# Head of a graph-attention kernel: weight, adjacency and x transfers put in another order

## What is computed

```python
def _L0_gnn_ref(h, adj, W, a):            # h = layernorm(x), W 128x128, a 1x256
    Wh = jnp.einsum('bni,oi->bno', h, W)
    a1 = a[0, :OUT_F]
    a2 = a[0, OUT_F:]
    si = Wh @ a1
    sj = Wh @ a2
    e = jax.nn.leaky_relu(si[:, :, None] + sj[:, None, :], negative_slope=ALPHA)
    attention = jnp.where(adj > 0, e, NEG_INF)
    attention = jax.nn.softmax(attention, axis=-1)
    h_prime = jnp.einsum('bij,bjo->bio', attention, Wh)
    return jax.nn.elu(h_prime)
...
x = x + _L0_gnn_ref(_layernorm(x, axis=-1), adj, L0_gnn_W, L0_gnn_a)
x = x + _L0_ffn_ref(_layernorm(x, axis=-1), ...)   # router per batch, top 2 of 8 experts, gelu, W1, W2
```

## Time and profile before

| | us |
|---|---|
| median of 3 runs | 276.9 |
| lowest and highest run | 275.93, 277.78 |
| the profiled execution's own time | 276.77 |
| its span, first to last instruction | 275.0 |

### The profile page before, as it was taken

How to read it: one execution, slowest core, us unless ns; L and a number is a source line. 1 busy time by engine, 2 the same in 40 slices (tenths; PEclk the granted TensorE clock), 3 DMA queues, 4 the chain that set the end, 5 groups by cost and what they waited for, 6 DMA issues and landing times. The chain is left out here.

```text
span 275.0 us, 6287 instructions
## 1 busy us (share of the span) xinstructions
PE 250.4 (91%) x1872; PEld 222.7 (81%) x1874; DVE 231.0 (84%) x647; ACT 223.4 (81%) x511; POOL 153.6 (56%) x228
## 2 busy tenths in 40 slices
PE   6878988998899899999989789999999999999980
PEld 3557977898889888899979457999999999999980
DVE  5589999999999999999999774587777777777774
ACT  2467898999999999999999659669888888888731
POOL 3435197778876697787468711164433333344544
PEclk9999999999999999999999999999999999999996
DMA  6999566643565346541000014678555545453122
GB/s 99 195 237 215 109 99 114 109 77 76 88 114 97 66 76 112 76 60 19 4 0 4 0 49 163 191 180 282 193 175 166 179 158 182 163 169 99 42 76 78
DMA packets 40706, 31.57 MB, mean 115 GB/s; under 512 B 2416, under 2 KB 36624, under 8 KB 40672
## 3 DMA queue, kind: packets, MB, share of 16 engines
q1 hardware_dynamic: 31936, 21.72, 24.7%
q0 software_dynamic: 8736, 9.45, 23.3%
HBM read 27.48 MB, written 4.20 MB: 115 GB/s over the span
## 5 line engine op out<-in xcount | busy, mean ns | idle before, releaser
L1253 PE MATMUL banks<-whx,prob_t 128*128 128x129 f32 x512 | 67.7, 277 | 2.7 <-ACT h_att L977 2.5
L1253 PEld LDWEIGHTS banks<-whx,prob_t 128*128 128x128 f32 x512 | 61.7, 192 | 5.5 <-issue 5.4
L383 POOL TENSOR_SCALAR x_all<-x_all,rstd,nb 128x128 f32<-128x128 f32 x56 | 41.0, 743 | 2.9 <-POOL nb L372 2.7
L1131 ACT ACTIVATE logit<-logit,nb,rstd 128x128 f32<-128x128 f32 x60 | 24.8, 484 | 19.3 <-POOL nb L448 19.3
L1005 ACT ACTIVATE prob_t<-banks 128x512 f32<-128x512 f32 x64 | 38.0, 637 | 2.7 <-PE banks L1238 2.7
L1238 PE MATMUL banks<-ident,logit 128*128 128x128 f32 x256 | 36.9, 275 | 3.5 <-DVE logit L533 3.3
L443 POOL TENSOR_SCALAR veps<-mv 128x4 f32<-128x4 f32 x15 | 6.7, 448 | 51.6 <-DVE mv L837 51.6
L366 POOL TENSOR_TENSOR rstd<-var,minus_half 128x8 f32<-128x8 f32 (+1 forms) x20 | 34.8, 1738 | 0.4
L1238 PEld LDWEIGHTS banks<-ident,logit 128*128 128x128 f32 x256 | 29.0, 141 | 5.9 <-DVE logit L533 5.6
L1415 PEld LDWEIGHTS banks<-w2s,masked_even 128*128 128x128 f32 x256 | 29.8, 192 | 0.7
L1415 PE MATMUL banks<-w2s,masked_even 128*128 128x128 f32 x256 | 29.9, 275 | 0.0
(11 more groups left out here) (149 smaller groups left out, 569.6 us busy)
## 6 DMA issues: line engine op xcount, KB each, us to landing
adj_sb<-in_adj_dram POOLq DMA_DIRECT2D x16, 512.0 KB, 7.0
w_pair<-w_parts SPq DMA_DIRECT2D x30, 256.0 KB, 2.4
x_all<-in_x_dram SPq DMA_DIRECT2D x16, 256.0 KB, 3.1
w2r<-in_L_ffn_W_dram SPq DMA_DIRECT2D x32, 128.0 KB, 2.1
out_dram<-prob_t SPq DMA_DIRECT2D x15, 256.0 KB, 2.3
w_parts<-in_L_ffn_W_dram SPq DMA_DIRECT2D x1, 1024.0 KB, 7.3
b_mix<-b_spread POOLq DMA_DIRECT2D x1, 704.0 KB, 5.8
out_dram<-prob_t SPq DMA_DIRECT2D x4, 64.0 KB, 1.7
```

Source lines behind the costliest of these rows:

```text
L383: nc.gpsimd.tensor_scalar(x_all[:, b, tile], x1_all[:, b, tile], rstd12[c % 4][:, 1, t:t + 1], nb2[c % 2][:, t:t + 1], ALU.mult, ALU.add). ...
L1131: nc.scalar.activation(zn[par][:, tile], zs[par][:, tile], ACT.Identity, bias=nb3[par][:, t:t + 1], scale=rstd3[par][:, t:t + 1]).then_inc ...
L1253: last = nc.tensor.matmul(into[:, 0:D + 1], prob_t[:, t, c * P:(c + 1) * P], whx[b % 3][:, c, 2:WHX], start=(c == 0), stop=(c == T - 1))
```

## The change

1. `a_src` and `a_dst` become two columns of one tile `a_both`, loaded by one transfer of 128x2 single elements, and that transfer is SP's first, ahead of W.
2. POOL issues adj0 as its first instruction, ahead of the constants; `load_adj(0)` ahead of `norms(0)` goes.
3. SP issues x2 when the prepared weights are ready (`s_prep`) and no longer behind adj0's landing; x3 still waits for that.
4. W1's load moves from behind x5 to behind x7, the small loads from behind x7 to behind x9, and the four `split_w1_hi` on ACT from steps 4 to 7 to steps 6 to 9.
5. In DVE's hand-written start, logits(0, 0) comes ahead of mask(1), and logits(0, 1) ahead of the first maximum of batch 1.
6. PE: for batch 0 `spread_dst` waits for each tile of `whx` by itself and not for all four; the fillers go from 8 to 6 at the start and from 5 to 3 behind `project(0)`.

```diff
--- before.py
+++ after.py
@@ -57,8 +57,8 @@
         idle_in = sb("idle_in", [P, N], BF16)
         minus_half = sb("minus_half", [P, T])
         gnn_w_sb = sb("gnn_w_sb", [P, D])
-        a_src = sb("a_src", [P, 1])
-        a_dst = sb("a_dst", [P, 1])
+        a_both = sb("a_both", [P, 2])
+        a_src, a_dst = a_both[:, 0:1], a_both[:, 1:2]
         w_stats = sb("w_stats", [P, 6])
         w_mean = sb("w_mean", [P, 2])
         gnn_w_centred = sb("gnn_w_centred", [P, D])
@@ -266,20 +266,21 @@
                 sp.dma_start(b1_sb[:], b1).then_inc(s_rw, 16)
                 sp.dma_start(b2_sb[:], b2).then_inc(s_rw, 16)
 
+            sp.dma_start(a_both[:], gnn_a.rearrange("a (k d) -> d (a k)", k=2),
+                         allow_slow_non_contiguous=True).then_inc(s_gw, 16)
             sp.dma_start(gnn_w_sb[:], gnn_w).then_inc(s_gw, 16)
-            sp.dma_start(a_src[:], gnn_a[0:1, 0:D].rearrange("a d -> d a")).then_inc(s_gw, 16)
-            sp.dma_start(a_dst[:], gnn_a[0:1, D:2 * D].rearrange("a d -> d a")).then_inc(s_gw, 16)
             load_x(0)
             load_x(1)
+            sp.wait_ge(s_prep, 1)
+            load_x(2)
             sp.wait_ge(s_adj[0], 16)
-            load_x(2)
             load_x(3)
             for b in range(4, B):
                 sp.wait_ge(s_mask, b - 3)
                 load_x(b)
-                if b == 5:
+                if b == 7:
                     sp.dma_start(w1_parts[:, :, 1, :].bitcast(F32), w1.rearrange("e p f -> p e f")).then_inc(s_w1raw, 16)
-                if b == 7:
+                if b == 9:
                     load_small()
 
             def load_w1(b):
@@ -325,6 +326,7 @@
 
         @block.gpsimd
         def _(pool):
+            nc.gpsimd.dma_start(adj_sb[0][:], adj_dram[0]).then_inc(s_adj[0], 16)
             nc.gpsimd.memset(ident[:], 0.0).then_inc(s_ident, 1)
             pool.wait_ge(s_ident, 1)
             nc.gpsimd.affine_select(out=ident[:], in_=ident[:], compare_op=ALU.not_equal, fill=1.0, base=0,
@@ -398,7 +400,6 @@
                 if 0 <= n + 4 <= B - 1:
                     load_adj(n + 4)
 
-            load_adj(0)
             norms(0)
             load_adj(1)
             norms(1)
@@ -475,9 +476,9 @@
             for i in range(3):
                 nc.vector.memset(whx[i][:], 1.0).then_inc(s_dconst, 1)
 
-            dve.wait_ge(s_gw, 48)
+            dve.wait_ge(s_gw, 32)
             nc.vector.bn_stats(w_stats[:], gnn_w_sb[:]).then_inc(s_centre, 1)
-            nc.vector.tensor_scalar(a_src_scaled[:], a_src[:], 1.0 - ALPHA, None, ALU.mult).then_inc(s_centre, 1)
+            nc.vector.tensor_scalar(a_src_scaled[:], a_src, 1.0 - ALPHA, None, ALU.mult).then_inc(s_centre, 1)
             dve.wait_ge(s_centre, 1)
             nc.vector.bn_aggr(w_mean[:], w_stats[:]).then_inc(s_centre, 1)
             dve.wait_ge(s_centre, 3)
@@ -617,10 +618,10 @@
             shift_high(0)
             shift_low(0)
             stats1(2)
+            logits(0, 0)
             make_mask(1)
-            logits(0, 0)
+            logits(0, 1)
             masked_max(1, 0)
-            logits(0, 1)
             masked_max(1, 1)
             logits(0, 2)
             masked_max(1, 2)
@@ -1079,8 +1080,8 @@
             probs(1, 0)
             for n in range(1, B - 1):
                 step(n)
-                if 4 <= n < 8:
-                    split_w1_hi(n - 4)
+                if 6 <= n < 10:
+                    split_w1_hi(n - 6)
             probs(B - 1, 1)
             normalize(B - 2)
             exp_h(B - 2)
@@ -1207,10 +1208,12 @@
             def spread_dst(b):
 
 
-                pe.wait_ge(s_wh, T * b + T)
-                if b >= 1:
+                if b >= 1:
+                    pe.wait_ge(s_wh, T * b + T)
                     pe.wait_ge(s_md, T * b)
                 for t in range(T):
+                    if b == 0:
+                        pe.wait_ge(s_wh, t + 1)
                     last = nc.tensor.transpose(dst_ps[:, t * P:(t + 1) * P], whx[b % 3][:, t, 0:1].to_broadcast([P, P]),
                                                ident[:])
                 last.then_inc(s_dst, 1)
@@ -1281,18 +1284,18 @@
                     attend(n, 2)
 
             pe.wait_ge(s_dconst, 1)
-            keep_busy(8)
+            keep_busy(6)
             pe.wait_ge(s_dconst, 2)
             pe.wait_ge(s_const, 1)
             transpose_x(0)
-            pe.wait_ge(s_gw, 48)
+            pe.wait_ge(s_gw, 32)
             pe.wait_ge(s_centre, 4)
             nc.tensor.transpose(dst_ps[:, 2:D + 2], gnn_w_centred[:], ident[:])
-            nc.tensor.matmul(dst_ps[:, 0:1], gnn_w_centred[:], a_dst[:], start=True, stop=True)
+            nc.tensor.matmul(dst_ps[:, 0:1], gnn_w_centred[:], a_dst, start=True, stop=True)
             nc.tensor.matmul(dst_ps[:, 1:2], gnn_w_centred[:], a_src_scaled[:], start=True, stop=True).then_inc(s_prep_ps, 1)
             pe.wait_ge(s_prep, 1)
             project(0)
-            keep_busy(5)
+            keep_busy(3)
             spread_dst(0)
             transpose_x(1)
             keep_busy(2)
```

## The result

| | before | after |
|---|---|---|
| median of the runs, us | 276.75 (4 runs, 275.93 to 277.78) | 281.47 (4 runs, 280.45 to 284.46) |
| after / before | | 1.0175, 95% interval 1.0136 to 1.0214 |
| profiled execution, us | 276.8 | 281.57 |
| its span, us | 275.0 | 279.8 |
| mean granted TensorE clock | 0.992 | 0.986 |

The forecast was 275.2 us in a range of 273.9 to 277.6: wrong in size and in sign. Of the 4.8 us by which the profiled span is longer, 3.7 stand in the first 22 us.

The account below looks back on a forecast made before the run. VectorE was taken to bound the kernel, full from about 26 us, so only its start could gain. maximum(1,1) moving from 18.60 to 17.0 gave 1.6 us, other terms 0: 276.8 - 1.6 = 275.2 us, range 273.9 to 277.6.

Parts of the forecast that it names:

- The price: x0: First x load, now issued 0.92 us behind adj0: takes 3.9 us, landing at 5.6, 0.6 us later; ends 4.6 to 7.4.
- by turns: Queues alternating packet by packet on the DMA engines: x0 lands at 7.4 us, total 277.0 us instead of 275.2.
- the fillers, costed at nothing: TensorE's start: six fillers for eight end near 4.0 us, then idle until x0; cost put at nothing.
- (b): Rival at the first load: x0 starves behind adj0; 277.0 us for landing at 7.4, 278.4 for 8.8; chance 0.17.
- (c): Rival in batch 0: TensorE stays at its lower clock, 3.1 us more on the chain, 277.4 us total; chance 0.07.
- ScalarE does not bind: First batches: x1's leaky row comes at about 13.6 us, ahead of logits(0,0) at 14.2, so no wait.
- x0 + 11.4: Start of maximum(1,1): x0's landing plus 2.2, 7.3 (adj1's transfer) and 1.9 us, for x0 above about 5.2.
- adj0's issue: GpSimd's start: adj0 issued at 0.74 us in place of the identity's memset, 1.20 us sooner.
- x2's stall: VectorE's 1.11 us wait before x2's statistics: goes, as x2 lands near 10 to 12 us, needed at 13.4.
- adj1 as the next one late: At mask(1): adj1, issued at 7.8 us, lands at 15.1, and VectorE waits about 0.3 us.
- the merged weights: Sync's start: one transfer for two score columns issues x0 at 1.66 instead of 2.13 us; its landing costs nothing.
- W1 and the splits: Attention loop: W1's load and ScalarE's four splits two batches later, costed at 0; ends 0.3 us won or lost.

Follow-up runs that it names:

- b_adj_x0_first: Kernel before with adj0 as GpSimd's first instruction and x0 first on Sync, ahead of W and the score columns: 281.09 us, ratio 1.0168.
- a_adj_back: Changed kernel with adj0's load put back behind the identity, all other edits kept: 277.18 us, ratio 0.9991.
- a_adj_fill_back: Changed kernel with adj0 back behind the identity and the fillers back to 8 and 5: 276.72 us, ratio 0.9994.
- b_adj_first: Kernel before with nothing but adj0 as GpSimd's first instruction: 281.45 us, ratio 1.0140.
- b_fill_cut: Kernel before with only the fillers cut, 6 for 8 at the start and 3 for 5 behind the first projection: 277.25 us, ratio 1.0009.
- a_warm: Changed kernel with 24 fillers instead of 6 at the start, keeping TensorE busy until x0 lands: 281.55 us, ratio 1.0169.
- a_router: Changed kernel with 8 and 6 instead of 4 and 2 fillers in TensorE's idle stretches ahead of the router: 281.60 us, ratio 1.0170.
- a_adj_late: a_adj_fill_back with adj0 held until VectorE's second whx constant is written: 276.96 us, ratio 0.9984.
- c_late_router: Changed kernel with adj0 behind the second whx constant, fillers 8 and 5, and 8 and 6 ahead of the router: 275.61 us, ratio 0.9977.
- b_w1_later: Kernel before with only W1's load, its splits and the small loads two batches later: 276.78 us, ratio 1.0012.

## Why the prediction was wrong

**The failed step is "The price: x0".** I drew a straight line between a load issued 0.2 us behind an adjacency (2.9 us to landing) and one issued 2.3 us behind (5.7 us). The runs show no line there but nearly a step. Sync's loads by how long after adj0 they were issued:

| issued behind adj0 by | load, kernel | landing after |
|---|---|---|
| ahead, 0.5 us | x0, `b_adj_x0_first` | 2.6 us |
| ahead, 0.2 us | x0, `a_adj_back` | 3.0 us |
| 0.19 us | x0, before | 2.9 us |
| 0.3 us | x1, `a_adj_back` / `a_adj_fill_back` | 3.3 / 6.0 us |
| 0.39 us | a_dst, `b_adj_first` | 2.1 us |
| 0.49 us | x0, after | 6.7 us |
| 0.52 us | a_src, `b_adj_x0_first` | 4.6 us |
| 0.66 us | x1, before | 7.1 us |
| 0.86 us | x0, `b_adj_first` | 6.6 us |
| 0.96 us | x1, after | 7.7 us |
| 1.0 us | a_dst, `b_adj_x0_first` | 5.1 us |

Up to 0.2 us behind, a load is unharmed (a column takes 2.0 to 2.1 us in the kernel before); from 0.5 to 1 us it is held back for most of adj0's way, whatever its size. Between them it went either way. The line at 0.49 us gives 3.3 us, less than half of what was measured. My far point was x2, 2.3 us behind adj1. (I also misread it: 5.7 us is a later load's, x2 took 5.9. That moves the line by 0.1 us.) A nearer row was at hand: x1 of before, 0.66 us behind and 7.1 us to landing, and I had used it as an outer bound only.

This is the Trainium skill's rule of turns between queues (DMA: Bandwidth & Descriptors, "Queues, rings and completion order") in direction, and more than it in size: by turns I had x0 at 7.4 us, and it landed at 8.5.

**The second failed step is the fillers, costed at nothing.** "Six fillers are three quarters of the eight" was no argument: `b_fill_cut` shows the lower level with six and x0 on time. The chain from landing to spread took 6.7 us and not 4.2; from the first transpose on it is 6.5 us, and 4.2 in `a_warm` at the upper level, so 2.4 us are TensorE's. The Trainium skill (TensorE: Matmul & The Clock Gate, "Part 1: The HAM clock gate") has the lower level as the default, and as what the engine falls back to without activity; the 4.42 us of idle time ahead of the slow transposes agree with either, and the traces do not tell which of the two it was.

**The rivals were priced one at a time.** (b) was x0 starved, (c) the lower level, each at 277 to 278. But they come together: a late x0 lengthens the very idle stretch ahead of the slow transposes. x0 at 8.5, the chain of 4.2 and 2.4 for the lower level put the spread at 15.1 us (15.2 measured). My own 6.4 us from the first maximum to maximum(1,1), the wait for adj1 left out, then give 21.5: 2.9 us slower, 279.7 us. The first 22 us cost 0.8 us more than that, and 0.64 of them are VectorE's wait for the leaky row: "ScalarE does not bind" was wrong once the chain was late. The formula x0 + 11.4 would not have found this. It follows another path, through adj1, which is the last to end only in `a_warm`; there it gives 19.3, and 20.62 was measured, since adj1 took 8.5 us and not 7.3.

**adj0's issue** at 0.74 us was wrong by half a microsecond: GpSimd's queue takes its first DMA at 1.27 us, in `b_adj_first` and `b_adj_x0_first` too, although a memset starts at 0.74. That made adj0 later, and x0's fate no better.

**Right** were: full VectorE from maximum(1,1) on, with the gap carried through the stage; x2's stall, which goes; adj1 as the next one late when the chain is fast (1.04 us in `a_warm`); the merged weights, whose landing of 2.2 us nobody waits for; W1 and the splits within their ends (0.3 us lost in the traces). The gain of the other edits, 1.5 us at maximum(1,1) in `a_adj_fill_back` for 1.6 forecast, is right by luck: adj0 is in its old place there, and its landing and not adj1's ends last.

**Open**: of the 4.75 us, 3.74 are at maximum(1,1) and shown. 0.35 more gather up to the end of attention, the price of moving W1 and the splits by the traces, without a wait that I could name. The last 0.65 lie at the router's spell in the profiled execution, but filling the gap (`a_router`) did not shorten the run. So that this spell explains the last part of the median is argued, not shown, and the same holds for the other runs of `a_warm`.

## What to carry to other kernels

Before a large GpSimd load is moved ahead, list every small load that another queue issues within the next microsecond or two: here those issued 0.5 us or more behind it landed nearly with it, and moving it *behind* them cost nothing, since it then took 6.0 us for 7.9 (7.3 in another kernel). When a load gets later, ask at once what level TensorE will be at when it lands, and follow both through the chain together; here fillers up to the landing gave the upper level back. A gain that one trace shows in the first 20 us need not be seen in the median: 2 us of it here came out as 0.2 to 0.5% of the time, 1.5 us as nothing.

## What I had not expected of the hardware

- Nearly a step, not a slope, in what a load on Sync's queue suffers from an adjacency load on GpSimd's: 2.9 us at 0.19 us behind, 6.7 us at 0.49, and either at 0.3.
- The adjacency issued later landed sooner: mask(0) at 9.26 us with adj0 issued at 3.31, at 10.09 with 2.75.
- GpSimd's first DMA starts at 1.27 us, its first memset could at 0.74.
- TensorE worked batch 0 at 1.2 GHz after six fillers and 0.78 us of idle time (`b_fill_cut`), and after eight and 3.81 us (`b_adj_first`, granted clock 0.54); it did not after eight and 0.45. Eight give no fixed outcome either: with no idle time behind them the transposes took 0.64 us in `a_adj_late`, 0.83 in `c_late_router`, and 1.06 in `b_w1_later` and `b_adj_x0_first`.
